# Decoder layer on one core: the score maxima turned by two products instead of eight, one bias moved to a copy, the others added once over 256 columns

## The chip, the cores and the metric

The kernel runs on one core of a Trainium2 chip. The metric is the time of one execution in device microseconds. The kernel before was run three times: 1312.6, 1320.65 and 1324.02 us, median 1320.65.

TensorE's clock has two levels, 1.2 and 2.4 GHz. The trace gives the granted clock of a stretch as a share of the higher one, so 1.00 is 2.4 GHz and 0.50 is 1.2 GHz.

## The reference

Sixteen sequences of 256 tokens with 128 channels pass through three sublayers, each followed by a residual sum and a layer norm:

- **Self-attention** with 16 heads of 8 channels. Queries, keys and values are `relu(x @ W + b)`. Scores are divided by sqrt(8), masked (causal, and padded keys), and go through a softmax. The result plus x is normalised with gamma and beta.
- **Cross-attention** over 64 context tokens of 96 channels, with no biases.
- **A feed-forward stack** of two blocks. Each block is a layer norm, a causal 16-head attention `x = x + softmax(q k) v @ wo + bo` with `q = h @ wq + bq`, `k = h @ wk + bk`, `v = h @ wv + bv`, and then a mixture of eight experts of which two are used: chosen per token in the first block, per sequence in the second.

What the change touches is the softmax's maxima, and the biases `bv` and `bo` of the attentions. Softmax weights of a row sum to one, so adding `bv` to the values or to the attention's output gives the same result in the feed-forward attentions, which have no query mask.

## The kernel before

**Units.** The attention work is 64 units, each one sequence in one stage: 16 of kind "self" (0 to 300 us), 16 of kind "ctx" (300 to 440 us), 16 of kind "ffn" for the first feed-forward block (440 to 740 us), and 16 "ffn" for the second (925 to 1190 us). Between the two ffn stages the experts of the first block run over 46 tiles. After the last ffn stage come the experts of the second block. Neither expert part is touched.

**Order.** All five engines issue an order that is written out by slots (`interleave`). A new self or ffn unit starts every 12 slots, a new ctx unit every 7. Each stage function (`pe_scores`, `pe_maxima` and so on) is a generator that starts in a slot relative to its unit's first slot and has a rank. A `yield` ends its part of the slot. Within a slot the lower rank is issued first. Nothing is reordered later: an engine that waits holds up all that is queued behind it.

**One unit's work.** Tokens are transposed on TensorE (slot -19, L546), copied by ScalarE (L792 or L794), projected to queries and keys (slot -16, L563 and L567), copied by ScalarE (L807, L811), split in two parts by VectorE (L989, L997), and laid out in other rows by DMAs that SyncE issues (L457, L471, L475). From slot 0 on there are 12 score rounds (4 for ctx): TensorE fills one of three banks (L614, L619, L624 to L630), VectorE takes the negated maximum of each row and head (L1010, L1014, L1018). Then the weights are computed a second time in transposed form (`pe_attend`, slot 17, L665, L673, L678). Their exponential is taken by ScalarE (L859), the causal mask is applied by GpSimd (L1170), and the products with the values follow (L698, L709, L716). The outputs are transposed (L728), divided by their sums on VectorE (L1055, L1060), and in ffn units transposed once more (`L736`), copied by ScalarE (L874), multiplied by `wo` (L742), given the bias `bo` (L743), and added to the residual (L1105).

**The maxima.** The softmax's maximum enters the second computation of the weights as eight more rows (96 to 103) of the queries. VectorE writes each maximum as a high and a low part into `maxparts`, 32 numbers per token (L1033, L1035). TensorE turns them (`pe_maxima`, from slot 13, rank 2, L648): for each half, four products against the identity, one for every group of heads and every tile of 128 tokens, each with a stationary operand of 104 columns, so that the eight numbers come out in rows 96 to 103 of the bank. ScalarE copies a half (8 rows by 512) into the queries (`act_maxima`, L840). The second half is issued one slot later, and since both halves use the same bank (`tokens`) in self and ffn units, it waits until ScalarE has copied the first. In ctx units the halves use two different banks. `pe_attend` of the unit waits for both copies.

**The bank `tokens`.** It is taken in turn by the two halves of the maxima (slots 13 and 14), by the value projection of a later unit (`pe_values_in`, slot 15 modulo the 12, L582 and L583), by the transposes and by the projections. Each user waits at `take` until the one before has been read out. ScalarE's order around the maxima is: exponential of slot 13, first copy, exponential of slot 14, second copy, exponential of slot 15, copy of the values (L829).

**Biases.** `bv` of the self and ffn attentions and `bo` are added by products of a matrix of ones with a two-row split of the bias (high and low part), one product of 128 columns for each tile of 128 tokens: `L583` and `L743`.

## Time and profile before

| | |
|---|---|
| Times | 1312.6, 1320.65, 1324.02 us; median 1320.65 |
| Profiled execution | span 1327.3 us; the page gives no other time for it |
| TensorE busy | 1215.2 us (92%), weight loads 990.1 us (75%), 9884 products |
| VectorE, ScalarE, GpSimd busy | 926.7 us (70%), 803.1 us (61%), 710.5 us (54%) |
| Chain that ended last | TensorE 66%, VectorE 13%, issue 5%, SyncE's queue 5%, ScalarE 4%, DMA 4%, GpSimd 3% |
| Mean granted clock | 0.958 |
| L648, the turning of the maxima | 512 products, 73.8 us busy (55.4 into `tokens`, 18.4 into the score banks) |
| L840, ScalarE's copies of them | 128 copies, 578 ns each |
| L583, bias of the values | 96 products; L743, bias `bo`: 64 products |
| L874, copy of the attention's output | 32 copies, 373 ns each |

"Busy" is the time in which an instruction of the engine is in flight. Weight loads (PEld) are a row of their own and overlap with products. The share of the span is an average over stages with different limits, so each stage has to be read by itself: what matters in it is which wait ends last.

### The profile page before, as it was taken

The numbers are of one execution on the slowest core, as the hardware profiler recorded it, in microseconds if no ns is written. First come the engines' busy times: TensorE is split into PE (matmuls) and PEld (weight loads), VectorE is DVE, ScalarE is ACT, GpSimd is POOL, SyncE is SP. The second block draws the span as 40 slices with busy tenths as digits, with TensorE's granted clock in tenths as the row PEclk, the third lists the DMA queues.
The fourth block names the chain that finished last, engine by engine and source line by source line (L and its number), as shares of the span: only waits on it lengthen the run. The fifth ranks groups of instructions, "written<-read, shape, count | busy, mean of one in ns | idle before, by whom it ended". The sixth has DMA issues, their size and how long they took to land.

```text
span 1327.3 us, 30592 instructions
## 1 busy us (share of the span) xinstructions
PE 1215.2 (92%) x9884; PEld 990.1 (75%) x9884; DVE 926.7 (70%) x2791; ACT 803.1 (61%) x1629; POOL 710.5 (54%) x1279
## 2 busy tenths in 40 slices
PE   4999999998887699999999899999999999989996
PEld 3777777766665477777777799898677777769996
DVE  6799999988777779989985221125788888635553
ACT  4566666775665366666666556564666666654552
POOL 4455555664231156777778431332677775445654
PEclk9899999998898799999998899999899999979998
DMA  4788776425666354555442787786565565255773
GB/s 118 218 230 239 221 225 185 125 71 155 167 168 163 94 141 127 128 131 136 120 118 63 225 231 232 229 254 209 140 154 146 152 155 148 79 156 166 213 201 103
DMA packets 208291, 216.94 MB, mean 163 GB/s; under 512 B 46403, under 2 KB 157507, under 8 KB 208132
## 3 DMA queue, kind: packets, MB, share of 16 engines
q1 hardware_dynamic: 191088, 193.49, 54.0%
q0 software_dynamic: 6304, 14.43, 3.9%
q10 hardware_dynamic: 10740, 7.06, 1.7%
q8 instruction: 80, 1.31, 0.4%
q14 instruction: 79, 0.65, 0.2%
HBM read 126.90 MB, written 85.46 MB: 160 GB/s over the span
## 4 chain that ended last, share of the span: by engine, by line
PE 66%; DVE 13%; issue 5%; SPq 5%; ACT 4%; DMA 4%; POOL 3%; POOLq 0%; DVEq 0%; ACTq 0%
PE scores L619 6%; PE weights L1573 6%; PE values L709 5%; PE weights L673 5%; PE scores L1831 4%; PE weights L678 4%; PE weights L1847 4%; PE values L716 3%; PE scores L1557 3%; PE scores L628 3%; DVE negmax L1014 3%; SPq L475 3%; DMA windows<-parts 2%; PE tokens L648 2%; PE tokens L582 2%
## 5 line engine op out<-in xcount | busy, mean ns | idle before, releaser
L1170 POOL TENSOR_SCALAR_AFFINE_SELECT probs<-probs 128x256 f32<-128x256 f32 (+1 forms) x576 | 279.5, 490 | 228.7 <-ACT probs L859 225.4
L859 ACT ACTIVATE probs<-weights 128x512 f32<-128x512 f32 x448 | 264.9, 598 | 120.3 <-PE weights L673 86.8
L1014 DVE TENSOR_REDUCE negmax<-scores 128x4 f32<-128x512 f32 x384 | 261.3, 685 | 86.2 <-PE scores L619 83.2
L619 PE MATMUL scores<-keys,queries 128*128 128x512 f32 (+1 forms) x384 | 186.1, 487 | 6.0 <-issue 1.7
L859 ACT ACTIVATE probs<-weights,keybias 128x512 f32<-128x512 f32 x192 | 131.5, 688 | 64.3 <-PE weights L673 48.0
L673 PE MATMUL weights<-queries,keys 104*128 104x256 f32 x768 | 159.0, 290 | 1.0 <-issue 0.6
L673 PEld LDWEIGHTS weights<-queries,keys 104*128 104x128 f32 x768 | 139.9, 194 | 22.3 <-issue 3.6
L1018 DVE TENSOR_REDUCE negmax<-scores 128x2 f32<-128x512 f32 (+1 forms) x192 | 131.0, 686 | 29.2 <-PE scores L625 19.4
L678 PEld LDWEIGHTS weights<-queries,keys 104*128 104x128 f32 x768 | 114.8, 195 | 10.2
L678 PE MATMUL weights<-queries,keys 104*128 104x128 f32 x768 | 110.2, 268 | 0.0
L709 PE MATMUL values<-probs,v 128*32 128x256 f32 x1536 | 106.6, 396 | 3.5 <-POOL probs L1170 3.5
L1573 PEld LDWEIGHTS weights<-out_room,probs 128*128 128x128 f32 x736 | 97.3, 193 | 7.3 <-DVE probs L1608 2.6
L619 PEld LDWEIGHTS scores<-keys,queries 128*128 128x128 f32 (+1 forms) x384 | 74.2, 194 | 37.6 <-issue 28.4
L1573 PE MATMUL weights<-out_room,probs 128*128 128x128 f32 x736 | 98.1, 277 | 2.2 <-DVE probs L1608 2.2
L1608 DVE TENSOR_TENSOR probs<-weights,hidden_room 128x256 f32<-128x256 f32 x46 | 19.5, 423 | 97.1 <-PE weights L1573 93.8
L1879 ACT ACTIVATE probs<-scores,out_room 128x256 f32<-128x256 f32 x128 | 53.6, 471 | 51.9 <-PE scores L1831 51.9
L648 PE MATMUL tokens<-ident_r,maxparts 128*104 128x128 f32 x384 | 55.4, 268 | 20.5 <-ACT queries L840 12.1
L1246 POOL DMA_INDIRECT routed_rows<-routed,slot_index x64 | 65.0, 1015 | 12.9 <-issue 12.9
L648 PEld LDWEIGHTS tokens<-ident_r,maxparts 128*104 128x104 f32 x384 | 44.2, 174 | 36.3 <-ACT queries L840 23.0
L1831 PE MATMUL scores<-srcT,hidden_room 128*128 128x256 f32 x256 | 69.3, 396 | 0.3 <-DMA hidden_room<-in_m_b 0.3
L716 PE MATMUL values<-probs,v 128*32 128x128 f32 x1536 | 63.2, 283 | 6.7 <-POOL probs L1170 6.1
L1847 PEld LDWEIGHTS weights<-out_room,probs 128*128 128x128 f32 x512 | 66.7, 192 | 3.2
(285 smaller groups left out, 2747.1 us busy)
## 6 DMA issues: line engine op xcount, KB each, us to landing
windows<-parts SPq DMA_DIRECT2D x192, 192.0 KB
queries<-windows SPq DMA_DIRECT2D x64, 384.0 KB
hidden_room<-in_m_w SPq DMA_DIRECT2D x78, 256.0 KB, 3.1
out_room<-in_m_w SPq DMA_DIRECT2D x78, 256.0 KB, 3.2
keys<-windows SPq DMA_DIRECT2D x192, 96.0 KB
routed_rows<-zeros SPq DMA_DIRECT2D x64, 256.0 KB, 3.6
windows<-parts SPq DMA_DIRECT2D x64, 120.0 KB
expert_rows<-probs ACTq DMA_DIRECT2D x46, 128.0 KB, 3.1
```

Source lines behind the costliest of these rows:

```text
L619: i = pe.matmul(bank[:], queries[0:rows, s, t * P:(t + 1) * P], keys[0:rows, s::S4, half * P:(half + 1) * P], start=True, stop=True)
L648: i = pe.matmul(X[0:MREND, k * T + t * P:k * T + (t + 1) * P], maxparts[g % 2][:, t, 8 * s:8 * s + MREND], ident_r[:], start=True, stop=True)
L673: i = pe.matmul(bank[:, k * T:(k + 1) * T], keys[0:MREND, S4 * a + s, 0:P], queries[0:MREND, s, :], start=True, stop=True)
L678: i = pe.matmul(bank[:, a * P:(a + 1) * P], keys[0:MREND, S4 * a + s, P:T], queries[0:MREND, s, P:T], start=True, stop=True)
L709: i = pe.matmul(OB[32 * a:32 * a + 32, (s % 2) * T:(s % 2 + 1) * T], values[:, 0, S4 * s + a, :], place(r - 3 + 2 * (s % 2) + a // 2)[:, ( ...
L859: act.activation(probs[:, n % RING], weight_banks[n % 2][:], ACT.Exp, scale=SCALE, **bias).then_inc(exp_done.sem, 1)
L1014: i = dve.tensor_reduce(most[:, part, s, :], bank[:].rearrange("p (a k) -> p a k", k=P), AX.X, ALU.max, negate=True)
L1018: i = dve.tensor_reduce(most[:, t, s, heads], bank[:].rearrange("p (a k) -> p a k", k=P * (t + 1)), AX.X, ALU.max, negate=True)
L1170: pool.affine_select(out=block, in_=block, compare_op=ALU.is_ge, fill=0.0, base=0, pattern=[[0, heads], [1, P]], channel_multiplier=-1).th ...
L1573: i = pe.matmul(y[:, t * C:(t + 1) * C], hidden_of[j % LANES][:, c, t * P:(t + 1) * P], out_w[j % WEIGHTS][:, c, :], start=(c == 0), stop= ...
L1831: i = pe.matmul(hidden_banks[n % 3][:, k * T:(k + 1) * T], hidden_w[lane][:, e, c * P:(c + 1) * P], srcT[lane][:], start=True, stop=True)
L1847: i = pe.matmul(y_banks[e][:, t * C:(t + 1) * C], g_of[lane][:, e, c, t * P:(t + 1) * P], out_w[lane][:, e, c, :], start=(c == 0), stop=(c ...
```

## The change

The maxima are turned by two products for each unit, one for each tile of 128 tokens. Each has all 128 columns of `maxparts` as its stationary operand. The columns are laid out anew: group s of heads at 32s, with the four high parts and then the four low parts. So the eight rows of group s come out in rows 32s to 32s+7, all in one half of the bank, and ScalarE copies them with four instructions (8 rows by 256 columns each), two in the slot of the first half and two in the slot of the second. There is one signal `maxT_ready` for each unit instead of two; `maxrows_placed` still counts two. In ctx units one bank is used instead of two.

`bv` of the ffn units is no longer added on TensorE. It is added as a per-partition bias in ScalarE's copy of the transposed attention output. It is loaded by two DMAs of its own, in ScalarE's queue. In self units `bv`, and in ffn units `bo`, is added by one product over 256 columns instead of two over 128.

```diff
         def pe_values_in(pe, g):
...
                 for t in range(NT):
-                    cols = slice(t * C, (t + 1) * C)
-                    pe.matmul(X[:, cols], src[:, t * P:(t + 1) * P], U.wv[:], start=True, stop=False)
-                    i = pe.matmul(X[:, cols], ones2[:], U.bv2[:], start=False, stop=True)
+                    i = pe.matmul(X[:, t * C:(t + 1) * C], src[:, t * P:(t + 1) * P], U.wv[:], start=t == 0, stop=U.kind != "self",
+                                  skip_group_check=True)
+                if U.kind == "self":
+                    i = pe.matmul(X[:, 0:NT * C], ones2[:], U.bv2[:, None, :].to_broadcast([P, NT, C]),
+                                  start=False, stop=True, skip_group_check=True)
...
-        def maxima_bank(g, half):
-            return context_banks[1 + half] if units[g].kind == "ctx" else tokens_bank
+        def maxima_bank(g):
+            return context_banks[1] if units[g].kind == "ctx" else tokens_bank

         def pe_maxima(pe, g):
             pe.wait_ge(maxparts_ready.sem, maxparts_ready.at(g))
-            for half in range(2):
-                bank = maxima_bank(g, half)
-                X = bank.tensor
-                bank.take(pe)
-                for k in range(2):
-                    s = 2 * half + k
-                    for t in range(NT):
-                        i = pe.matmul(X[0:MREND, k * T + t * P:k * T + (t + 1) * P], maxparts[g % 2][:, t, 8 * s:8 * s + MREND],
-                                      ident_r[:], start=True, stop=True)
-                i.then_inc(maxT_ready.sem, 1)
-                bank.until(maxrows_placed.sem, maxrows_placed.at(g, half + 1))
-                yield
+            bank = maxima_bank(g)
+            bank.take(pe)
+            for t in range(NT):
+                i = pe.matmul(bank.tensor[:, t * P:(t + 1) * P], maxparts[g % 2][:, t, :], ident_r[:], start=True, stop=True)
+            i.then_inc(maxT_ready.sem, 1)
+            bank.until(maxrows_placed.sem, maxrows_placed.at(g, NT))
+            yield
...
         def pe_outputs(pe, g):
...
-                    cols = slice(t * C, (t + 1) * C)
-                    pe.matmul(X[:, cols], aoT[:, t * P:(t + 1) * P], U.wo[:], start=True, stop=False)
-                    i = pe.matmul(X[:, cols], ones2[:], U.bo2[:], start=False, stop=True)
+                    pe.matmul(X[:, t * C:(t + 1) * C], aoT[:, t * P:(t + 1) * P], U.wo[:], start=t == 0, stop=False, skip_group_check=True)
+                i = pe.matmul(X[:, 0:NT * C], ones2[:], U.bo2[:, None, :].to_broadcast([P, NT, C]), start=False, stop=True,
+                              skip_group_check=True)
...
         def act_maxima(act, g):
             act.wait_ge(stacked.sem(g), stacked.at(g))
+            X = maxima_bank(g).tensor
+            act.wait_ge(maxT_ready.sem, maxT_ready.at(g))
             for half in range(2):
-                X = maxima_bank(g, half).tensor
-                act.wait_ge(maxT_ready.sem, maxT_ready.at(g, half + 1))
-                act.copy(Q[g % LANES][MROW:MREND, 2 * half:2 * half + 2, :],
-                         X[MROW:MREND, :].rearrange("p (s t) -> p s t", s=2)).then_inc(maxrows_placed.sem, 1)
+                for s in (2 * half, 2 * half + 1):
+                    i = act.copy(Q[g % LANES][MROW:MREND, s, :], X[32 * s:32 * s + 8, 0:T])
+                i.then_inc(maxrows_placed.sem, 1)
                 yield
...
         def act_outputs(act, g):
...
-                act.copy(aoT[:], mixed[:, 0:T]).then_inc(aoT_taken.sem, 1)
+                act.activation(aoT[:], mixed[:, 0:T], ACT.Identity, bias=U.bv[:]).then_inc(aoT_taken.sem, 1)
...
         def dve_scores(dve, g):
...
-                dve.wait_ge(maxT_ready.sem, maxT_ready.at(g - 2, NT))
-            parts = maxparts[g % 2][:, :, MROW:P].rearrange("p t (s h a) -> p t s h a", s=S4, h=2)
-            high, low = parts[:, :, :, 0, :], parts[:, :, :, 1, :]
+                dve.wait_ge(maxT_ready.sem, maxT_ready.at(g - 2))
+            parts = maxparts[g % 2][:].rearrange("p t (s r) -> p t s r", s=S4)
+            high, low = parts[:, :, :, 0:S4], parts[:, :, :, S4:2 * S4]
```

The rest of the diff loads `l0_bv` and `l1_bv` as columns and takes them out of `BIAS_ROWS`, so the two casts that split the bias rows at the start (L1339, L1342) cover 512 numbers instead of 768.

## Rows read from the trace of the kernel before

**Rows 1.** Windows: us, busy PE, PEld, DVE, ACT, POOL, clock, DMA share, GB/s

```profile
151.50:168.00 16.50, 16.32 (x149) 12.89 (x148) 14.93 (x43) 11.58 (x21) 9.68 (x21) 1.00 0.78 219
345.00:350.00 5.00, 4.42 (x23) 3.39 (x24) 2.43 (x8) 1.58 (x4) 1.90 (x3) 0.50 0.75 212
350.00:400.00 50.00, 41.65 (x323) 32.20 (x322) 36.65 (x124) 31.67 (x68) 13.80 (x28) 0.92 0.62 169
550.00:600.00 50.00, 46.31 (x428) 37.04 (x428) 44.72 (x141) 31.91 (x67) 39.45 (x65) 1.00 0.52 130
1050.00:1100.00 50.00, 48.52 (x447) 36.85 (x445) 43.36 (x103) 33.45 (x67) 36.07 (x60) 1.00 0.61 147
```

**Rows 2.** Chain of waits, one self unit: start us, us, what

```profile
151.75 0.25 PE weights L673 x2
152.02 0.69 ACT probs L859
152.76 0.59 ACT queries L840
153.39 0.58 PE tokens L648 x4
...
168.25 0.25 PE weights L673 x2
```

**Rows 3.** Timeline, the same unit: start us, us, what, idle before

```profile
152.08 0.44 PEld L648 LDWEIGHTS tokens<-ident_r,maxparts 128*104 128x104 f32 x4 [0.30 <-DVE maxparts L1035]
152.44 0.19 PEld L628 LDWEIGHTS scores<-keys,queries 96*128 96x128 f32 x1
153.36 0.69 ACT L859 ACTIVATE probs<-weights,keybias 128x512 f32<-128x512 f32 x1
153.39 0.44 PEld L648 LDWEIGHTS tokens<-ident_r,maxparts 128*104 128x104 f32 x4 [0.29 <-ACT queries L840]
154.08 0.58 ACT L840 CAST queries<-tokens 8x512 fp32r<-8x512 f32 x1
154.71 0.30 PEld L582 LDWEIGHTS tokens<-a_wv,srcT 128*128 128x128 f32 x2
155.37 0.19 PEld L628 LDWEIGHTS scores<-keys,queries 96*128 96x128 f32 x1
```

**Rows 4.** Timeline, two copies of 256 columns back to back on ScalarE

```profile
158.81 0.35 ACT L790 CAST keeprows<-tokens 2x256 fp32r<-2x256 f32 x1
159.06 0.36 ACT L794 COPY srcT<-tokens 128x256 f32<-128x256 f32 x1
```

**Rows 5.** Chain of waits, shares by line, 310 to 400 us

```profile
by line: SPq L475 30.5%; DMA windows<-parts 24.9%; SPq L457 14.6%; issue 6.4%; SPq L471 6.0%; DVE negmax L1010 4.4%; DVE res L920 1.3%; PE weights L665 1.2%; DVE ao L1055 1.0%; DVE stats_last L899 0.9%; PE scores L614 0.8%; DVE parts L993 0
```

**Rows 6.** Waits: total us, times, longest; span, 500 to 700, 960 to 1160 (twice)

```profile
PEld tokens L648 <- ACT queries L840: 23.0, 46, 0.9
...
PEld tokens L546 <- DVE tok L920: 7.9, 10, 1.4
...
PEld tokens L648 <- DVE maxparts L1035: 3.1, 10, 0.4
PEld mixed L742 <- ACT aoT L874: 2.4, 12, 0.2
```

**Rows 7.** Timeline, one unit of the second ffn stage

```profile
1039.83 0.58 ACT L840 CAST queries<-tokens 8x512 fp32r<-8x512 f32 x1 [0.19 <-PE tokens L648]
1041.71 0.30 PEld L582 LDWEIGHTS tokens<-l_wv,srcT 128*128 128x128 f32 x2
```

**Rows 8.** Groups by line and form: count, busy us, mean ns, idle before

```profile
L807 ACT ACTIVATE queries_keys_taken<-tokens,l_bq 128x256 f32<-128x256 f32 x32 | 15.2, 474 | 25.2 <-PE tokens L567 25.2
L874 ACT COPY aoT<-mixed 128x256 f32<-128x256 f32 x32 | 11.9, 373 | 25.5 <-PE mixed L736 25.5
```

**Rows 9.** Timeline, the first ffn unit, TensorE at the lower clock

```profile
455.49 0.44 PEld L648 LDWEIGHTS tokens<-ident_r,maxparts 128*104 128x104 f32 x4 [2.14 <-DVE maxparts L1035]
458.23 0.50 PEld L582 LDWEIGHTS tokens<-l_wv,srcT 128*128 128x128 f32 x2 [0.64 <-ACT queries L840]
```

More of the change, by code:

```diff
@@ L83, with __init__ @@
 class Unit:
-    def __init__(self, kind, wq, wk, wv, wo=None, bq=None, bk=None, bk2=None, bv2=None, bo2=None, ln_w=None, ln_b=None):
+    def __init__(self, kind, wq, wk, wv, wo=None, bq=None, bk=None, bk2=None, bv=None, bv2=None, bo2=None, ln_w=None, ln_b=None):
         self.kind, self.n, self.attend, self.groups = kind, ROUNDS[kind], ATTEND[kind], PV_GROUPS[kind]
@@ L225, in decoder, with as_column @@
                      (("stats", [6]), ("meanvar", [2]), ("vareps", []), ("rstd", []))] for n in ("pre", "post", "last", "route")}
+        def as_column(n):
+            return ins[n].rearrange("o c -> c o") if n[2:] == "_bv" else ins[n]
         w, first, late, slow = {}, [], [], []
@@ L231, in decoder @@
             w[n] = const(n, [CC, C])
-        for n in ("a_bq", "l0_bq", "l0_bk", "l0_ln1_w", "l0_ln1_b"):
+        for n in ("a_bq", "l0_bq", "l0_bk", "l0_bv", "l0_ln1_w", "l0_ln1_b"):
             w[n] = const(n, [P, 1])
@@ L236, in decoder @@
         for n in w:
-            (first if n[:2] == "a_" else late).append((w[n][:], ins[n].to_broadcast([P, C]) if n in ("a_gamma", "a_beta") else ins[n]))
+            (first if n[:2] == "a_" else late).append((w[n][:], ins[n].to_broadcast([P, C]) if n in ("a_gamma", "a_beta") else as_column(n)))
         for k in range(2):
@@ L260, in decoder @@
         w["m1_gb"] = const("m1_gb", [1, E])
-        late += [(w[n][:], ins[n]) for n in list(w) if n[:2] in ("l1", "m1") and n[-6:] != "_parts" and n[3:5] != "gw" or n[:5] == "m0_ln"]
+        late += [(w[n][:], as_column(n)) for n in list(w) if n[:2] in ("l1", "m1") and n[-6:] != "_parts" and n[3:5] != "gw" or n[:5] == "m0_ln"]
         slow.append((w["m1_gw"][:], ins["m1_gw"]))
@@ L312, in decoder @@
             of = lambda name: w[f"l{n}_{name}"]
-            units += [Unit("ffn", of("wq"), of("wk"), of("wv"), wo=of("wo"), bq=of("bq"), bk=of("bk"), bv2=of("bv_parts"),
+            units += [Unit("ffn", of("wq"), of("wk"), of("wv"), wo=of("wo"), bq=of("bq"), bk=of("bk"), bv=of("bv"),
                            bo2=of("bo_parts"), ln_w=of("ln1_w"), ln_b=of("ln1_b"))] * B
```

8 lines of the change are left out of this document (4 added, 4 removed).

## The prediction

> **What bounds the kernel now.** I read the windows first, one for each stage, because the page's 92% for TensorE is a mean. A self unit repeats every 16.50 us, and TensorE is busy for 16.32 of them at full clock, VectorE for 14.93 [rows 1]. The first ffn stage has TensorE at 46.3 of 50 us and VectorE at 44.7, the second 48.5 and 43.4. The ctx stage has nobody full: 41.7 and 36.7 [rows 1].
>
> Next the chain of waits, stage by stage. In the self stage it stays on TensorE all the way, except for one excursion: the weights of slot 13 end, ScalarE takes their exponential, copies the first half of the maxima, and only then does TensorE turn the second half. The same weights stand 16.50 us later [rows 2]. In the ctx stage 75% of the chain is SyncE's issues at L475, L457 and L471 and the DMA between them [rows 5]: TensorE's work there is under another limit. In the first ffn stage ten units out of the eleven or twelve in 200 us have TensorE's transposes wait for VectorE's tokens (L920) [rows 6]: VectorE's routing and reductions set the pace, in a part of the unit where the maxima are not on the chain. In the second ffn stage ten units in 200 us have the maxima themselves wait for VectorE's `maxparts` [rows 6], so the loop is VectorE up to `maxparts`, then the maxima, then the value projection, then TensorE.
>
> Last the timeline around the maxima. Before the second half TensorE sits idle for 0.29 us [rows 3], over the kernel 23.0 us in 46 of the 48 units that share the bank [rows 6]. The value projection L582 then starts at 154.71, and ScalarE's second copy ends at 154.08 + 0.58 = 154.66 [rows 3]. A semaphore takes about 0.05 us from ScalarE to TensorE (the first copy ends at about 153.34, L648 starts at 153.39 [rows 2, 3]). So L582, which takes the same bank, starts at the first moment at which it could. This coincidence decides the case.
>
> **The change on TensorE.** Four turnings take 152.44 - 152.08 = 0.36 us, 0.09 each [rows 3]; six instructions of L582 and L583 take 155.37 - 154.71 = 0.66, 0.11 each [rows 3]. Two wide turnings are two of the latter kind, 0.21. Each unit saves 0.72 - 0.21 = 0.51 us of TensorE, 33 us over 64 units. A bias product over 256 columns I take at 0.12 (L673 on the chain: 0.25 for two of that width [rows 2]) against 0.21 for two narrow ones: 0.09 saved in each self unit (`bv`) and each ffn unit (`bo`). The two L583 of an ffn unit go: 0.21, or 6.7 us over 32. Together 33 + 1.4 + 2.9 + 6.7 = 44 us of TensorE's work, and with the 23.0 us of idle time before the second half, 67 us. Little of it arrives.
>
> **Where it goes in a self unit.** The second half no longer waits, so TensorE comes to L582 about 0.36 + 0.15 + 0.29 = 0.8 us sooner, at 153.9. But L582 takes `tokens`, which ScalarE now frees after its second pair of copies. ScalarE's path: the exponential of slot 13 starts at 152.02 as before, since it waits for weights that stand ahead of the maxima in the order. Then comes the first pair, the exponential of slot 14, and the second pair. What is new is the length of a pair of 8x256 copies against one 8x512 copy of 0.58. The trace has two such copies without a wait between them: the second starts 0.25 after the first, which lasts 0.35, and lasts 0.36 itself [rows 4]. A pair is 0.61, 0.03 more than one wide copy. With no overlap it would be 0.72, 0.14 more; below 0.58 it would have to be faster than one copy of as many columns, which I exclude. I take 0.03, the row nearest in kind. L582 then starts 2 x 0.03 = 0.06 later than now and its bias ends 0.09 sooner: 0.03 us off a unit at best, I take 0.02. The wait has moved from L648 to L582 and grown by what was saved. Queued behind L582 are the scores and weights of slot 16, so nothing on TensorE gets round it. Fifteen periods: -0.3 us.
>
> By the Trainium skill ("ScalarE: Activation LUTs", What ACT_TABLE_LOAD costs) an activation with immediate operands takes 186 + 0.833 N ns and neighbours overlap by about 93: a pair would be 0.71 and one wide copy 0.61, 0.09 more and not 0.03. By that figure the sum below would be about 4 us higher. The measured wide copy is 0.58 and the measured pair 0.61, and the trace decides.
>
> **Ffn units on TensorE's own loop.** These are six of the first stage (before and after the ten that follow VectorE) and four of the second: the copies cost nothing as above, the two L583 behind L582 save 0.21, `bo` 0.09. Against them the copy L874 becomes an activation with a bias column: 0.47 instead of 0.37 [rows 8], and TensorE's L742 waits for it already, 12 times by 0.2 [rows 6], so 0.10 comes on top. Net -0.2 a unit: -2.0 us for ten.
>
> **The ten VectorE units of the first ffn stage: 0.** Maxima, values and `bo` lie beside VectorE's part of the loop. What covers them is VectorE's routing; without that cover they would be worth the 0.2 above.
>
> **The second ffn stage, twelve units.** ScalarE sat idle 0.19 before the first copy, waiting for L648 [rows 7]. Two turnings are done 0.15 sooner; ScalarE's path to L582 is then 0.15 shorter and 0.06 longer: L582 starts about 0.1 sooner than 1041.71 [rows 7], and without L583 what follows is 0.32 sooner. The loop runs on through VectorE to the next `maxparts`, which moves with it. L874 is in VectorE's part here, off the chain. 12 x -0.32 = -3.8 us.
>
> **Starts of stages at the lower clock.** In the first ffn unit L648 starts at 455.49 and L582 at 458.23, waiting for ScalarE, with no exponential between the copies [rows 9]. Afterwards: 0.46 to the first copy, 0.61 twice, 0.05, so 457.2; 1.0 sooner, and 0.4 more for two L583 at half speed. I take four such units (the first of the self stage, of ctx, the last of ctx, this one) at -1.0 each. Bounds: 0 if the DMAs behind them end at the same time, -1.4 each. -4.0 us.
>
> **At nothing:** the ctx stage proper, covered by SyncE's queue (if that cover went, 0.5 us a unit, -6); the two new DMAs on ScalarE's queue, which issue between exponentials in slots away from the maxima; VectorE's casts into `maxparts`, same size; the two set-up casts, shorter by a third, worth up to -0.5.
>
> Sum: -0.3 - 2.0 - 3.8 - 4.0 = -10.1 us. The profiled execution has a span of 1327.3, 0.5% above the median of the runs and above the slowest of them. On its own terms it becomes 1317; on the median's, 1320.65 - 10 = 1311.
>
> **Rivals.**
>
> *A, the freed TensorE time arrives (1276).* If L582 does not wait for ScalarE, a self unit saves 0.9 (15 x 0.9 = 13), the ten ffn units about 0.9 more each (9), and the twelve units 1.0 more each (12): 34 more than my sum. For it: TensorE carries most of the chain, and VectorE leaves 1.5 us free in a self unit [rows 1]. Against it: the order of ScalarE's slots and the 0.05 us in [rows 3].
>
> *B, the pair of copies does not overlap (1319).* 0.14 instead of 0.03 is 0.22 more for each of 37 units, +8: almost no change. For it: the copies move data from rows 0, 32 and 64 to row 96, which no row shows. Against it: [rows 4].
>
> *C, slower: the granted clock falls in the ffn stages (1349).* TensorE had 46.3 of 50 us busy in the first ffn stage with the clock at 1.00, but 41.7 in the ctx stage with 0.92, and 0.50 in a stretch with a long DMA wait [rows 1]. The change takes 0.8 us of work from each ffn unit of about 17, which leaves 44 of 50. If the ffn stages fell to the 0.86 between those two levels, TensorE's parts of their loops (about 7 us in ten units of the first, 10 in the second and in the rest) would stretch by a sixth: 10 x 1.2 + 16 x 1.6 = +38, and 1311 + 38 = 1349. It outweighs the gain from a clock of about 0.96 down. Against it: in the self stage the new wait is about 1 us, and TensorE has gaps of that size now at 1.00. The Trainium skill speaks for it ("Perfetto Trace Analysis", Matmul Optimizations): the engine scales its power with utilization, so products should follow each other back to back; it gives no number for this case.
>
> **Chances.** Forecast 0.65, with a range of its own of 1303 to 1318 (stage starts 0 to -5.6, pair 0.03 to 0.08, spread of a median of three); A 0.14; B 0.13; C 0.08. The time is 1311. The range 1288 to 1325 takes in B, the upper noise and cases half-way to A, and leaves out A in full and C. This kernel's measurement can tell about 1%, 13 us, from no change: below 1307.4 lie A and a quarter of the forecast (0.16), so faster 0.31; slower C and little else, 0.10; within 1%, 0.59.
>
> **What would show it.** Right: in the self stage L582 waits about 1 us for L840 in each unit, L648 for nothing but `maxparts`, and the period stays within 0.1 of 16.50. The first ffn stage keeps VectorE as its limit; the second shortens by about 0.3 a unit. TensorE's busy time falls by some 40 us and the span by 10. Wrong: a self period under 16.2 (A), a gap of more than 0.66 between the start of a pair of copies and its end (B), or a granted clock under 0.98 in 550 to 600 or 1050 to 1100 us (C).

## The result, and the profile after

The kernel after takes 1350.51 us (median of 4 runs, 1346.77 to 1354.36) against 1317.76 for the kernel before in the same session: ratio 1.0238, 95% interval 1.019 to 1.0285. It is slower by 33 us, and the prediction, 1311 with 1288 to 1325, was wrong in its sign as well. The time is close to that of rival C (1349).

The page of the profiled execution, its span, the busy times, the granted clock in 40 slices, and the chain's shares by engine:

```profile
span 1345.1 us, 29730 instructions
PE 1200.0 (89%) x9388; PEld 966.4 (72%) x9388; DVE 925.6 (69%) x2791; ACT 825.4 (61%) x1757; POOL 709.7 (53%) x1279
PEclk9999999996987689987889899999998999899998
PE 66%; ACT 9%; DVE 8%; issue 6%; POOL 4%; SPq 4%; DMA 3%; POOLq 0%; ACTq 0%; DVEq 0%
```

TensorE issues 496 products fewer and is busy only 15 us less, in a longer span. ScalarE's share of the chain went from 4% to 9%. The mean granted clock is 0.926, before 0.958.

The windows of the kernel after that answer to [rows 1], and at the end four neighbouring ones of 10 us (us, busy PE, PEld, DVE, ACT, POOL, clock, DMA share, GB/s):

```profile
550.00:600.00 50.00, 47.05 (x401) 36.26 (x398) 41.10 (x126) 31.59 (x66) 35.07 (x59) 0.88 0.48 120
1050.00:1100.00 50.00, 45.61 (x410) 34.88 (x408) 42.82 (x99) 34.75 (x73) 35.20 (x60) 1.00 0.66 154
500.00:700.00 200.00, 183.85 (x1516) 144.27 (x1515) 168.24 (x534) 126.08 (x267) 139.06 (x230) 0.87 0.47 119
950.00:1150.00 200.00, 180.91 (x1599) 136.61 (x1598) 166.72 (x387) 134.93 (x281) 135.47 (x229) 0.97 0.59 144
570.00:580.00 10.00, 9.82 (x97) 7.71 (x96) 8.52 (x24) 6.98 (x14) 7.34 (x13) 1.00 0.48 116
580.00:590.00 10.00, 8.95 (x53) 6.86 (x55) 7.07 (x28) 5.27 (x13) 6.67 (x11) 0.62 0.59 150
590.00:600.00 10.00, 9.94 (x91) 7.86 (x92) 7.78 (x21) 6.30 (x12) 6.26 (x11) 0.87 0.27 71
600.00:610.00 10.00, 8.95 (x52) 7.03 (x51) 7.62 (x29) 5.34 (x13) 7.05 (x12) 0.65 0.56 151
```

The same two long windows of the kernel before:

```profile
500.00:700.00 200.00, 184.83 (x1721) 147.59 (x1720) 180.87 (x574) 129.10 (x260) 150.85 (x248) 0.99 0.49 126
950.00:1150.00 200.00, 193.72 (x1773) 148.66 (x1771) 168.00 (x390) 134.23 (x264) 132.94 (x228) 1.00 0.58 145
```

The clock fell from 0.99 to 0.87 in the first ffn stage. TensorE's busy time hardly moved there (184.8 and 183.9 us) although 205 products fewer got done. About 100 of them are the removed ones (nine in each of some 11 units), and the rest did not get their turn in the 200 us, since each takes longer at the lower level. That is the trap of a busy share: here it did not fall when the clock did. The last four windows show a period: for about 10 us of each unit the clock is at the lower level, then it is back.

Waits of TensorE's weight loads over the span (total us, times, longest), and the timeline of one self unit, which answers to [rows 3] (start, us, engine, line, ..., idle before):

```profile
PEld tokens L585 <- ACT queries L842: 54.4, 44, 1.6
...
PEld tokens L650 <- DVE maxparts L1037: 13.2, 27, 2.1
```

```profile
149.68 0.69 ACT L861 ACTIVATE probs<-weights,keybias 128x512 f32<-128x512 f32 x1 [0.71 <-PE weights L674]
149.74 0.30 PEld L650 LDWEIGHTS tokens<-ident_r,maxparts 128*128 128x128 f32 x2 [0.31 <-DVE maxparts L1037]
...
150.39 0.73 ACT L842 CAST queries<-tokens 8x256 fp32r<-8x256 f32 x2
151.15 0.69 ACT L861 ACTIVATE probs<-weights,keybias 128x512 f32<-128x512 f32 x1
151.86 0.74 ACT L842 CAST queries<-tokens 8x256 fp32r<-8x256 f32 x2
152.62 0.69 ACT L861 ACTIVATE probs<-weights,keybias 128x512 f32<-128x512 f32 x1
152.65 0.52 PEld L585 LDWEIGHTS tokens<-a_wv,srcT 128*128 128x128 f32 x4 [1.11 <-ACT queries L842]
```

L585 is the value projection (L582 before). The 23.0 us of waiting in the turning [rows 6] are gone and 54.4 us stand in the value projection. It starts when the second pair of copies ends. A pair takes 0.73 to 0.74 us, where one wide copy took 0.58.

The same stretch at the lower clock, in a unit of the first ffn stage: the four products of L585 take 1.22 us; in a unit of the self stage at full clock they take 0.71.

```profile
602.98 1.22 PE L585 MATMUL tokens<-l_wv,srcT 128*128 128x128 f32 x4 [1.05 <-ACT queries L842]
```

**By stages**, from the starts of ScalarE's copies of the outputs (L868 before, L870 after), us:

| | to the first output | self | ctx | first ffn | tiles | second ffn | rest |
|---|---|---|---|---|---|---|---|
| before | 61.0 | 244.9 | 143.0 | 287.9 | 214.3 | 235.3 | 141.0 |
| after | 57.8 | 250.2 | 143.0 | 305.2 | 208.0 | 241.9 | 138.9 |

The profiled execution of before lies 0.7% above the median and that of after below its own, so the difference here is 18 us and not 33; 6 us of the gap are in the experts' tiles, in work that the change does not touch. The loss is in the self stage (+5) and the two ffn stages (+17, +7). In the self stage eleven periods of 16.50 us became nine of 16.67 and two of 18.23; in the first ffn stage four units take 20.0 to 20.5 us where they took 17.5; in the second the undisturbed period is 15.86 (15.91 before), but five units are longer by 1.5 to 2.8. Each of these eleven long units (two, four and five) holds a stretch at the lower level, and together they are 24 of the 29 us that the three stages lost. The time at the lower clock level, read from the trace's record of the clock, is 114.7 us before and 201.6 after. Of the 87 us more, 62 lie in the first ffn stage (25.1 and 86.8), 14 in the second, 6 in the self stage, and 20 in the ctx stage, which takes 143.0 us in both; outside the four stages the kernel after has 15 us less.

### The profile page after: what moved, and what is told of

It reads as the page before. It is cut to its first block, busy times and chain, and to the rows that moved or that the text cites. A ratio compares the mean times of both kernels' runs of the same rounds, so it can differ in the third digit from the quotient of the medians.

```text
span 1345.1 us, 29730 instructions
## 1 busy us (share of the span) xinstructions
PE 1200.0 (89%) x9388; PEld 966.4 (72%) x9388; DVE 925.6 (69%) x2791; ACT 825.4 (61%) x1757; POOL 709.7 (53%) x1279
## 3 DMA queue, kind: packets, MB, share of 16 engines
q8 instruction: 76, 1.25, 0.4%
## 4 chain that ended last, share of the span: by engine, by line
PE 66%; ACT 9%; DVE 8%; issue 6%; POOL 4%; SPq 4%; DMA 3%; POOLq 0%; ACTq 0%; DVEq 0%
PE values L710 6%; PE scores L625 6%; PE weights L1575 6%; PE weights L674 5%; PE values L717 4%; PE scores L1833 4%; ACT queries L842 4%; PE weights L1849 4%; PE weights L679 4%; ACT probs L861 3%; PE scores L1559 3%; PE scores L634 3%; PE tokens L585 3%; PE tokens L567 2%; SPq L479 2%
## 5 line engine op out<-in xcount | busy, mean ns | idle before, releaser
L625 PE MATMUL scores<-keys,queries 128*128 128x512 f32 (+1 forms) x384 | 194.1, 509 | 5.1 <-ACT queries L842 1.7
L674 PE MATMUL weights<-queries,keys 104*128 104x256 f32 x768 | 163.3, 296 | 1.2 <-issue 0.9
L674 PEld LDWEIGHTS weights<-queries,keys 104*128 104x128 f32 x768 | 146.4, 203 | 23.3 <-issue 4.1
L679 PEld LDWEIGHTS weights<-queries,keys 104*128 104x128 f32 x768 | 119.0, 202 | 13.0 <-ACT probs L861 2.5
L710 PE MATMUL values<-probs,v 128*32 128x256 f32 x1536 | 117.5, 429 | 3.6 <-POOL probs L1172 3.5
L679 PE MATMUL weights<-queries,keys 104*128 104x128 f32 x768 | 114.4, 274 | 1.9 <-ACT probs L861 1.9
L625 PEld LDWEIGHTS scores<-keys,queries 128*128 128x128 f32 (+1 forms) x384 | 78.9, 207 | 42.4 <-issue 30.6
L1575 PE MATMUL weights<-out_room,probs 128*128 128x128 f32 x736 | 97.1, 275 | 0.8 <-DVE probs L1610 0.8
L842 ACT CAST queries<-tokens 8x256 fp32r<-8x256 f32 x192 | 69.5, 362 | 15.2 <-PE tokens L650 11.6
L1849 PE MATMUL weights<-out_room,probs 128*128 128x128 f32 x512 | 67.0, 275 | 0.0
```

Of the source, the lines that this page charges most:

```text
L625: i = pe.matmul(bank[:], queries[0:rows, s, t * P:(t + 1) * P], keys[0:rows, s::S4, half * P:(half + 1) * P], start=True, stop=True)
L674: i = pe.matmul(bank[:, k * T:(k + 1) * T], keys[0:MREND, S4 * a + s, 0:P], queries[0:MREND, s, :], start=True, stop=True)
L679: i = pe.matmul(bank[:, a * P:(a + 1) * P], keys[0:MREND, S4 * a + s, P:T], queries[0:MREND, s, P:T], start=True, stop=True)
L710: i = pe.matmul(OB[32 * a:32 * a + 32, (s % 2) * T:(s % 2 + 1) * T], values[:, 0, S4 * s + a, :], place(r - 3 + 2 * (s % 2) + a // 2)[:, ( ...
L842: i = act.copy(Q[g % LANES][MROW:MREND, s, :], X[32 * s:32 * s + 8, 0:T])
L1575: i = pe.matmul(y[:, t * C:(t + 1) * C], hidden_of[j % LANES][:, c, t * P:(t + 1) * P], out_w[j % WEIGHTS][:, c, :], start=(c == 0), stop= ...
```

## The experiments

The numbered theories of the expectations: theory 1 lays the loss on the new wait at the value projection, the place where TensorE stands idle for about 1 us; theory 2 says that TensorE has less to do in its loop, so that its clock falls, wherever the idle time lies; theory 3 lays it on the bias products, or in the last set on ScalarE's pairs. Ratios are to runs of the kernel before on the same chip. "Lower level" is the time with the clock at 1.2 GHz in the profiled execution, and beside it stands the part of it in the first ffn stage. That is one execution for each kernel. Over all its executions in these experiments the mean clock of the kernel before lies between 0.948 and 0.967, which would be 87 to 137 us at the lower level; that of the kernel after lies between 0.916 and 0.932, e1 between 0.933 and 0.937, f5 between 0.928 and 0.940. Only these three lie clear of the kernel before; of the others none reads below 0.942, and differences of 20 us in the column between them are not told apart.

| kernel | median, us | ratio, 95% interval | clock | lower level, us | of it, first ffn stage | self period, us |
|---|---|---|---|---|---|---|
| before | 1317.8 to 1322.3 | | 0.958 | 114.7 | 25.1 | 16.50 |
| after | 1350.5 | 1.0238 (1.0190 to 1.0285) | 0.926 | 201.6 | 86.8 | 16.67 |
| e1, maxima part alone | 1354.8 | 1.0254 (1.0231 to 1.0277) | 0.937 | 173.3 | 42.4 | 16.78 |
| e2, bias part alone | 1317.0 | 0.9975 (0.9959 to 0.9991) | 0.958 | 113.8 | 25.6 | 16.39 |
| e3, after, copies together | 1311.3 | 0.9899 (0.9853 to 0.9944) | 0.948 | 139.2 | 29.2 | 16.18 |
| e4, after, more products | 1328.7 | 1.0061 (1.0040 to 1.0082) | 0.953 | 127.9 | 30.5 | 16.85 |
| f5, after, values earlier | 1336.3 | 1.0066 (1.0030 to 1.0103) | 0.928 | 195.5 | 77.1 | 16.20 |
| f6, before, values earlier | 1323.1 | 0.9992 (0.9970 to 1.0014) | 0.960 | 107.5 | 48.7 | 16.38 |
| f7, before, split copies | 1326.4 | 1.0036 (1.0006 to 1.0066) | 0.956 | 119.4 | 30.8 | 16.60 |
| g1, f5 and more products | 1324.9 | 1.0017 (0.9988 to 1.0046) | 0.950 | 135.6 | 54.4 | 16.20 |
| g2, e3 and more products | 1314.4 | 0.9944 (0.9917 to 0.9970) | 0.951 | 129.4 | 36.5 | 16.42 |
| g3, before, more products | 1338.9 | 1.0121 (1.0080 to 1.0161) | 0.970 | 82.7 | 24.7 | 17.07 |
| g4, after, eight turnings | 1343.4 | 1.0163 (1.0116 to 1.0210) | 0.957 | 116.5 | 22.4 | 17.24 |
| h1, e3 and more products in ffn | 1306.7 | 0.9889 (0.9840 to 0.9938) | 0.957 | 113.6 | 36.4 | 16.18 |

### e1 and e2: each part alone

e1 is the kernel before with only the new `maxima_bank`, `pe_maxima`, `act_maxima` and layout of `maxparts`; e2 has only the changes to `bv` and `bo`.

> The kernel before with the maxima's part of the change alone: two wide products, four copies of 8x256; the biases stay as they were. Theory 1 (the wait for the bank moves to the value projection, TensorE pauses there about 1.1 us in a block in each unit, and the granted clock falls): nearly the whole loss is here, 1340 to 1355 us, self period 16.7, clock of the whole run near 0.93. Theory 2 (fewer products in all make TensorE less active and lower the clock, wherever they are taken away): about three quarters of the loss, in proportion to the products removed (33 of 44 us of work), 1335 to 1345. Theory 3 (the bias in ScalarE's copy of the attention output costs it): no slower than before, about 1318.

> The bias parts of the change alone (bv of the ffn units in ScalarE's copy, bv of the self units and bo once over 256 columns); the maxima are turned by eight products in two halves as before. Theory 1: no loss, a gain of 1 to 6 us, 1312 to 1317, clock as before (0.96). Theory 2: a quarter of the loss, 1324 to 1328, clock 0.94 to 0.95. Theory 3: the whole loss, about 1345.

The loss is there with the maxima part alone: e1 has ratio 1.0254, with the clock at 0.937, and 1354.8 us is in the range of theory 1 and above that of theory 2. The bias part alone gains 0.25%, 3 us, with the clock unchanged, so the biases by themselves are out as a cause.

The two parts do not simply add, though. e1 loses 9 us in the self stage, 7 in the first ffn stage and 14 in the second, where the kernel after loses 5, 17 and 7. Its undisturbed periods are longer (16.78 us in the self stage and 16.43 in the second ffn stage, against 16.67 and 15.86), and it has only half as long at the lower level in the first ffn stage (42.4 us against 86.8). On top of the maxima part the bias part shortens the loop and goes with a lower clock, and the total comes out nearly the same.

### e3: ScalarE's four copies in one slot

```diff
             for half in range(2):
                 for s in (2 * half, 2 * half + 1):
                     i = act.copy(Q[g % LANES][MROW:MREND, s, :], X[32 * s:32 * s + 8, 0:T])
                 i.then_inc(maxrows_placed.sem, 1)
-                yield
+            yield
+            yield
```

> The changed kernel, but ScalarE makes all four copies of the maxima in one slot, ahead of the exponential of slot 14, so the bank is free about 0.7 us sooner. Theory 1: the value projection's wait for ScalarE falls from about 1.1 to 0.4 us a unit, the self period goes from 16.67 to about 16.1 at full clock, and the clock recovers in part: 1315 to 1335 us. Theory 2: the products are as few as in the changed kernel, so the clock stays at about 0.93 and only the period at full clock gains: 1338 to 1345.

The exponential of slot 14 no longer stands between the pairs, and `tokens` comes free about 0.7 us sooner. The time is 1311.3, 1% below the kernel before and 3% below the kernel after. The wait fell from 54.4 to 23.1 us, and most of the clock came back. The time lies 4 us below the range of theory 1 and far below that of theory 2, which had the clock stay. In e3's waits, its timeline and its windows:

```profile
PEld tokens L585 <- ACT queries L842: 23.1, 34, 1.3
```

```profile
164.98 1.50 ACT L842 CAST queries<-tokens 8x256 fp32r<-8x256 f32 x4
```

```profile
500.00:700.00 200.00, 179.93 (x1667) 142.13 (x1665) 177.41 (x585) 133.68 (x289) 156.66 (x255) 0.99 0.47 123
```

Four copies take 1.50 us, 0.37 each: they do not overlap here either. In 200 us TensorE does 151 products more than in the kernel after, in less busy time.

### e4: four more products in each self and ffn unit

```diff
                 elif U.kind == "ffn":
...
-                    i = pe.matmul(bank[:], queries[0:rows, s, t * P:(t + 1) * P],
+                    for _ in range(3 if r in (2, 3) else 1):
+                        i = pe.matmul(bank[:], queries[0:rows, s, t * P:(t + 1) * P],
```

(and in the same way in self units.) Two score products (rounds 2 and 3, 512 columns each) are issued twice more before the one that counts. The result is the same.

> The changed kernel with score rounds 2 and 3 of each self and ffn unit issued two more times into the same bank before the one that counts (four more products of 512 columns a unit, results unchanged). They stand just ahead of the value projection, where TensorE waits about 1.1 us for ScalarE, and take about 0.95 us of that. Theory 1 and theory 2 both say that more activity of TensorE raises the granted clock: if the clock is the cause, the run gets faster although TensorE has 45 us more to do, 1320 to 1335 us, clock over 0.95. If the loss were ScalarE's longer path alone, the time stays at 1345 to 1352 or gets longer.

More work made the kernel 22 us faster: 1328.7 against 1350.5, and the intervals of the ratios lie far apart. A score product of this width is 0.23 us on the chain, so the four add about 0.9 us to a unit, yet the self period rose only by 0.18, since most of it fills the wait before L585 (0.4 us in a self unit, 1.1 in the kernel after). So e4 adds products and shortens the wait at once, and does not say which of the two brings the clock back. The clock in e4's windows:

```profile
500.00:700.00 200.00, 185.92 (x1677) 147.72 (x1675) 180.74 (x575) 135.43 (x288) 151.78 (x249) 1.00 0.51 128
950.00:1150.00 200.00, 190.26 (x1693) 146.34 (x1693) 166.77 (x388) 137.33 (x285) 133.10 (x227) 1.00 0.58 144
```

### f5 and f6: the value projection four slots earlier

```diff
-    values_in = {"self": 3, "ffn": 3, "ctx": 0}
+    values_in = {"self": -1, "ffn": -1, "ctx": 0}
```

It now takes `tokens` before the maxima and waits for no copy. f5 does so in the kernel after, f6 in the kernel before.

> The changed kernel with the value projection of self and ffn units four slots earlier (slot -1 instead of 3), so it takes the bank before the maxima do and nothing takes it for four slots after them. Same products and copies. Theory 1 (the loss is the wait at the value projection, and the clock that falls with it): the wait for ScalarE is gone, self period 15.6 to 15.9 us, clock near 0.96, 1280 to 1300 us. Theory 2 (fewer products lower the clock by themselves): products as few as in the changed kernel, clock stays at 0.93 to 0.94, 1315 to 1335.

> The kernel before with the same move of the value projection, as the control of the run before: the second half of the maxima still waits for the first copy (0.3 us a self unit). Theory 1: the value projection waited for nothing here, so the time stays within 0.5% of before, 1314 to 1322; the whole gain of the pair belongs to the change once its wait is gone. Theory 2 says the same.

f6 takes the time of the kernel before, but it is not the same inside. In its profiled execution the first ffn stage takes 297.8 us instead of 287.9, with 48.7 us at the lower level instead of 25.1, and the other stages make up for it. No product is removed there and the value projection waits for no copy, so the order of the work alone can bring more of the lower level.

f5 is the run against theory 1. The wait for L842 is no longer among TensorE's nine largest, the self period is 16.20, and still the clock stays at 0.928 and the time at 1336.3, 1 us above the range of theory 2. It is 14 us faster than the kernel after all the same, with as long at the lower level; against its control f6 the change now costs 13 us and not 33. So a part of the loss hangs on the wait itself, without the clock. Other waits are there, in 500 to 700 us and 960 to 1160 us of f5, and its windows:

```profile
PEld tokens L550 <- DVE tok L922: 10.5, 10, 1.4
PEld mixed L769 <- DVE route_mask L1139: 9.3, 11, 1.0
```

```profile
PEld values L710 <- POOL probs L1172: 11.3, 11, 1.1
```

```profile
500.00:700.00 200.00, 179.11 (x1470) 139.84 (x1471) 166.20 (x524) 121.60 (x256) 137.56 (x227) 0.88 0.46 117
950.00:1150.00 200.00, 185.23 (x1566) 137.52 (x1558) 151.02 (x373) 129.74 (x271) 129.76 (x219) 0.92 0.54 140
```

The idle time of TensorE moved to its next waits, of about 1 us each. The eleven waits for `probs` in the second ffn stage come once per unit. Eight of its units take 17.2 us, each with a short stretch at the lower level; one between them without it takes 15.86.

### f7: the kernel before with each wide copy split in two

```diff
-                act.copy(Q[...][MROW:MREND, 2 * half:2 * half + 2, :], X[MROW:MREND, :].rearrange(...)).then_inc(...)
+                for k in range(2):
+                    i = act.copy(Q[...][MROW:MREND, 2 * half + k, :], X[MROW:MREND, k * T:(k + 1) * T])
+                i.then_inc(maxrows_placed.sem, 1)
```

> The kernel before, but each of ScalarE's two 8x512 copies of the maxima is made as two 8x256 copies. All eight products stay. It prices ScalarE's longer path alone: 2 x 0.15 us a unit in the self stage, so a self period of 16.8 and +4 to +10 us in all, 1324 to 1330, at a clock of 0.95 to 0.96 if a wait of 0.45 us at two places does not move it (theory 1). Theory 2: clock exactly as before, since no product is taken away. Were the split copies the cause of the clock's fall, the clock would read below 0.94 and the time above 1335.

It costs 0.36%, about 5 us (the interval starts at 0.06%), within the 1324 to 1330 expected, and leaves the clock alone. Its timeline shows what the prediction had wrong about the pair:

```profile
153.06 0.64 ACT L841 CAST queries<-tokens 8x256 fp32r<-8x256 f32 x2
...
154.43 0.63 ACT L841 CAST queries<-tokens 8x256 fp32r<-8x256 f32 x2
```

```profile
L841 ACT CAST queries<-tokens 8x256 fp32r<-8x256 f32 x192 | 60.9, 363 | 19.8 <-PE tokens L648 14.4 <-issue 1.8
```

Here both copies read rows 96 to 103 and write rows 96 to 103, and a pair takes 0.64: 192 copies of 363 ns have a union of 60.9 us, 0.32 each. In the kernel after the same instruction reads from rows 0, 32, 64 and 96 in turn:

```profile
L842 ACT CAST queries<-tokens 8x256 fp32r<-8x256 f32 x192 | 69.5, 362 | 15.2 <-PE tokens L650 11.6
```

192 copies of 362 ns take 69.5 us, 0.36 each: no overlap at all. Shape and types are the same. What differs is where they read: other start rows with the same columns of the bank in the kernel after, the same rows with other columns in f7. That the changing start row is what ends the overlap is the likely reading; it is not shown, since rows and columns were not varied one by one.

### g1 to g4: more products where there is no such wait, and the turnings put back

g1 is f5 with the edit of e4, g2 is e3 with it, g3 the kernel before with it. g4 is the kernel after with each turning product issued four times:

```diff
             for t in range(NT):
-                i = pe.matmul(bank.tensor[:, t * P:(t + 1) * P], maxparts[g % 2][:, t, :], ident_r[:], start=True, stop=True)
+                for _ in range(4):
+                    i = pe.matmul(bank.tensor[:, t * P:(t + 1) * P], maxparts[g % 2][:, t, :], ident_r[:], start=True, stop=True)
```

> The kernel after with its value projection sixteen slots... earlier (slot -1 of its unit, as in f5_values_early) and with the four extra score products per self and ffn unit of e4_filler. Nothing of the result is left out; the extra products are overwritten. Theory 2 (the granted clock falls when TensorE stands idle more, wherever the idle time lies): the time at the lower level returns from 195.5 us to below 130, the second feed-forward stage from 245 to about 235 us, and the time is 1305 to 1325, at or below f5's 1336. Theory 1 (only the wait at the value projection counts, and more products cost their own time): 60 extra us of products at some share, 1340 to 1380.

(The text for g1 speaks of sixteen slots and of 60 us of products; the projection is four slots earlier, as in f5, and 192 products of 0.23 us are 44 us.)

> The kernel after with ScalarE's four copies in one slot (as in e3_copies_together) and the four extra score products per self and ffn unit. e3 has its clock mostly back already (139 us at the lower level against 115 before). Theory 2: the filler takes the last 25 us at the lower level away, worth at most 12 us, but it lies where TensorE has no wait to fill now (the wait for ScalarE is down from 54 to 23 us), so it costs some 0.3 to 1.0 us in each of 48 units: 1315 to 1340, slower than e3's 1311. Theory 1: the same sign, 1330 to 1360.

> The kernel before with the same four extra score products per self and ffn unit, a control: what the filler costs where the clock is at its higher level already. The bank wait of 0.5 us per unit in the turning can take a part. 192 products at about 0.25 us are 48 us of work; with most of it on TensorE's own path 1345 to 1370. If this stays at 1320, the filler is free for another reason than the clock, and e4 says little on the clock.

> The kernel after with each of its two turning products issued four times (the result is the same), so that a unit has eight again, and ScalarE's pairs and the wait for them stay. Theory 2 (less of TensorE's work lets the clock fall): the time at the lower level goes from 202 us back to about 120, and the time is 1325 to 1335. Theory 3 (ScalarE's pairs of copies and the order around them let it fall, the number of products doesn't matter): low time stays 180 to 210 us, and the six products add up to 0.9 us per unit to the path, 1350 to 1385.

g3 is the price of the extra products where the clock is up already: +16 us, a little under the 1345 to 1370 expected. Of some 44 us of products a third arrives. In the kernel after the same edit gains 22 us (e4). g1 against f5 gains 11 by the medians and 6 by the ratios, whose intervals overlap; its mean clock, 0.942 to 0.955, lies above that of f5 in every execution. g1 is at the edge of what theory 2 expected: 1324.9 of 1305 to 1325, 135.6 us at the lower level and not below 130, 233.5 us in the second ffn stage where about 235 was expected. If the extra products cost the same 16 us there, 22 to 38 us came back with the clock. That is an estimate from above: in e4 and g1 they partly fill idle time that g3 does not have, and so cost less.

g4 puts back the number of turning products and leaves ScalarE's pairs in place. The clock returned as in the kernel before:

```profile
PEld tokens L585 <- ACT queries L843: 44.4, 43, 1.6
```

```profile
500.00:700.00 200.00, 182.98 (x1699) 146.75 (x1700) 179.74 (x580) 136.26 (x291) 151.30 (x250) 1.00 0.52 132
```

The lower level is 116.5 us instead of 201.6, with 43 waits of up to 1.6 us still at the value projection over the whole kernel. But this does not separate the wait from the number of products, as a look at the stages shows. The clock came back in the first ffn stage, 22.4 us at the lower level against 86.8, and there the wait became shorter too, since TensorE comes to it later by the six extra turnings. The value projection of one unit in the kernel after, just ahead of the dips that begin at 582 us, and of one in g4:

```profile
565.67 0.52 PEld L585 LDWEIGHTS tokens<-l_wv,srcT 128*128 128x128 f32 x4 [1.19 <-ACT queries L842]
```

```profile
571.13 0.52 PEld L585 LDWEIGHTS tokens<-l_wv,srcT 128*128 128x128 f32 x4 [0.81 <-ACT queries L843]
```

In the self stage the wait is nearly as long as in the kernel after (1.0 and 1.1 us), and so it is in the second ffn stage (1.25 in both), but there the kernel after had lost little of the clock (12 and 23 us at the lower level), and g4 has about the same (13 and 17). What separates the two a little is e1: its waits for ScalarE at the value projection in 500 to 700 us are longer than those of the kernel after (16.6 us for twelve, against 12.0 for ten), it has three products more in each ffn unit, and it has half as long at the lower level there.

g4 is 7 us faster than the kernel after by the medians, although its self period is 0.57 longer; the intervals of the ratios overlap. It is still 1.6%, 21 us, slower than the kernel before, with the clock of the kernel before. Its time missed the 1325 to 1335 of theory 2: in the second ffn stage two units still take 19.4 us around short stretches at the lower level, and the six extra turnings, which stand ahead of ScalarE's copies, lengthen the path in every unit (17.24 in the self stage, and 16.51 in the second ffn stage against 15.86).

g2, at 1314.4, is just under what theory 2 expected (1315 to 1340). With the copies together the extra products cost 3 us, which the intervals do not tell from nothing.

### h1: copies together, more products in the ffn units alone

> The kernel after with ScalarE's four copies in one slot, and the four extra score products in the 32 feed-forward units alone. The self stage is that of e3 (239.6 us, 16.18 per unit), the feed-forward stages those of g2 (285.1 and 232.5 us), against e3's 285.1 and 235.6: 3 us below e3's 1311, so 1306 to 1312 (theory 2, idle time of TensorE lets its clock fall). If the last wait of e3 costs no clock (theory 1), the extra products only add: 1313 to 1325.

1306.7 us, ratio 0.9889, in the range of theory 2. It is the fastest version here, but its interval overlaps that of e3, so whether the extra products add anything to e3 is not shown. Its lower level is 113.6 us, as in the kernel before. h1 and e3 beat both kernels.

## Why the prediction was wrong

**The clock** (rival C, given 0.08) is the large part. The step that failed is that the forecast priced everything at the clocks of the trace of before and took the lower level only at the starts of stages; in the ten units of the first ffn stage, put at nothing because VectorE covers them, and in the second ffn stage a fall of the clock had no term. What the runs showed in its place: the first ffn stage has 86.8 us at the lower level instead of 25.1 and takes 17 us longer, and the eleven units with a long period, all with such a stretch in them, are 24 of the 29 us that the three stages lost. e3, e4 and g4 against the kernel after, and g1 against f5, each give TensorE more to do or less to wait for. In each the clock rises and the median time falls, in g1 and g4 by less than the intervals can tell.

The share of the clock is an estimate from these periods. The whole times do not isolate it: g4 has the clock back and is still 21 us slower than the kernel before, with six turnings in the path of each unit that the kernel after does not have, and f5 gained 14 us without any of the clock. Both have other undisturbed periods than the kernel after.

The rival's direction was right: the change took work from TensorE that nothing replaced. Its measure was not: it expected TensorE's busy time to fall from 46.3 of 50 us to 44 [rows 1], and in 550 to 600 us it is 47.05 at a clock of 0.88. I gave it little because TensorE had gaps of 1 us at full clock already. That was a misreading for the self stage, where the longest idle time of TensorE's products before is 0.1 us, in 100 to 250 us. Gaps of that size there were in the first ffn stage, but two only (over 0.8 us, in 500 to 700 us), and the kernel after has twelve there. The rival's check was the one that spoke, in the first ffn stage alone: 0.88 in 550 to 600 us, and 1.00 in 1050 to 1100, where it was also asked for.

Its size: 1349 was worked out from 26 stretched units, a clock of 0.86 and a forecast of 1311. The 0.86 is said to lie between the two readings of [rows 1], but these are 0.92 and 1.00, and it lies under both; 0.96 would have made the stretch a quarter of what was taken and the time about 1321. What happened is fewer units and larger steps, 1.5 us for a unit with one short stretch and about 3 for one with 10 us at the lower level, on top of a base that the pairs had raised. That the total agrees is mostly luck.

**The pair of copies** (rival B, given 0.13) is the small part. The term "0.03 more than one wide copy" should have been 0.15. It came from two copies back to back with other shapes and the same start row [rows 4]. The prediction's "0.72 with no overlap" was the bound that held, and the check for B, more than 0.66, spoke as well, with 0.73 to 0.74. The estimate from the figures of the Trainium skill ("ScalarE: Activation LUTs", What ACT_TABLE_LOAD costs), 0.71 for a pair, was nearer than mine. But it comes from 0.40 for one copy and an overlap of 0.09, and this trace has 0.362 for one and no overlap; f7, where the copies do overlap, has 0.64. With 0.24 more on ScalarE's path and the rest of the step as predicted, the self period would be 16.72; it is 16.67. The second ffn stage was to shorten by 0.32 a unit and shortened by 0.05 in its undisturbed units, which is 0.27 less and close to the same 0.24.

**Right, on the place:** the value projection waits 1.1 to 1.25 us for ScalarE in each unit, L650 waits in self and ffn units for nothing but `maxparts`, and the freed time of TensorE did not arrive (rival A). The copy L876 with its bias takes 0.47 us, as priced. The ctx stage is unchanged at 143.0. The term for the starts of stages (-4.0) is not confirmed: the step to the first output of an ffn unit, priced at -1.0, is 1.3 us longer (33.05 instead of 31.75), and the time to the first output, 3.2 us shorter, ranges from 55.1 to 63.7 us over the kernels of the table. The bias part was small: e2's gain is 3 us, where its terms made 4.5 (2.0, and 0.21 in each of twelve units). The first ffn stage did not keep VectorE as its limit. In 500 to 700 us of the kernel after, the ten waits for VectorE's tokens [rows 6] are down to four:

```profile
PEld tokens L550 <- DVE tok L922: 3.7, 4, 1.4
```

Where the clock is low, TensorE sets the pace instead. (That e3 takes 1311 is no point for the forecast: it gets there by another order of the copies.)

**Not settled.** What in a unit decides between the levels. It is not the sum of TensorE's busy time, which is 179.9 us of 200 in e3 at a clock of 0.99 and 179.1 in f5 at 0.88. It is not the wait at the value projection alone: f5 has none of it and the clock stays low, and e1 has longer ones than the kernel after and half the time at the lower level in the first ffn stage. It is not the number of products alone: between e3 and the kernel after it is the same, and the lower level is 139 against 202 us, and f6 has all the products of the kernel before and twice its lower level in the first ffn stage. The runs say that fewer products and longer waits work in the same direction; they do not say how much of either it takes. A run that adds the removed products at a place where the wait keeps its length in the first ffn stage was not made. Nor do the runs say why the dips from 580 us on come back in every period.

## What to carry to other kernels

If TensorE sets the pace and stands idle for a little in each loop, removing its work can cost time, as it did here: read the granted clock of every stage before and after, and ask what will fill the time that is freed. Work taken from an engine whose next step waits for another engine can lengthen that wait and do no more; here moving ScalarE's copies ahead of one exponential (e3) was worth 39 us, and without it the removed products cost more than they saved. Price two short copies as two, unless the trace shows that pair, with those rows, overlapping.

## What the runs showed of the hardware

- Products whose result is thrown away made a kernel faster by 22 us (e4), with the mean clock from 0.926 to 0.953; they also fill a wait of 1.1 us. In the kernel before they cost 16 us.
- The clock can dip once per loop, in step with it: four units in a row at 20.0 to 20.5 us, each with about 10 us at the lower level. The longest idle time of TensorE's products in that stretch (500 to 700 us) is 1.35 us, and TensorE is busy for 183.9 of 200 us.
- The same products in another order can have twice the time at the lower level in a stage: 48.7 us in the first ffn stage of f6, 25.1 before, in one execution of each.
- Two 8x256 copies of ScalarE back to back take 0.64 us where both read rows 96 to 103 (f7) and 0.73 to 0.74 where each reads from another start row (after); four take 1.50 (e3). One alone is 0.36 in both.
- TensorE's busy time is no measure of its work when the clock falls: 183.9 us for 1516 products after, 184.8 for 1721 before, in the same 200 us.
